# Hop gathers in a graph network: the rows of each group split into two float32r parts for one 256-column product

## What is computed

```python
h = relu(layernorm(x))
msg = where(edge_type == 0, h[src] @ W_data.T + b_data, h[src] @ W_control.T + b_control)
x = x + relu(segment_sum(msg, dst) + h @ W_self.T + b_self)
h = relu(layernorm(x)); out = h
norm = deg_inv_sqrt[src] * deg_inv_sqrt[dst]
for _ in range(2):
    h = segment_sum(h[src] * norm[:, None], dst)
    out = out + h
return x + out / 3
```

## Time and profile before

| | us |
|---|---|
| median of 3 runs (lowest to highest) | 4009.13 (4006.95 to 4013.33) |
| the profiled execution | 4008.96 |
| its span, first to last instruction | 4007.0 |
| TensorE busy (products) | 3415.7 |
| VectorE busy | 2200.8 |
| ScalarE busy | 2418.7 |
| GpSimd busy | 2745.4 |

### The profile page before, as it was taken

One profiled execution on the slowest core, in us unless ns is written; L12 is line 12 of the kernel. 1 busy time (PEld: TensorE's weight loads), 2 busy tenths in 40 slices (PEclk: granted clock), 3 DMA queues, 4 the chain that ended last, 5 costly groups with the idle time before them and its releaser, 6 DMA issues.

```text
span 4007.0 us, 50989 instructions
## 1 busy us (share of the span) xinstructions
PE 3415.7 (85%) x17910; PEld 2466.8 (62%) x17910; DVE 2200.8 (55%) x3265; ACT 2418.7 (60%) x3174; POOL 2745.4 (69%) x2915
## 2 busy tenths in 40 slices
PE   7666777787777778777777899999998899999999
PEld 4344444444444444444444688888887688888887
DVE  7523888888988889898898422222222222122212
ACT  4001444454444445444444688888887788888887
POOL 2677777777777777777777576666664376666664
PEclk9788999899999999999999999999999999999999
DMA  6222443434343444444344566666666666666665
GB/s 194 86 60 61 119 116 110 133 110 125 109 126 109 115 129 117 118 117 117 110 133 109 168 185 190 192 189 191 190 191 182 179 184 182 181 181 182 186 182 145
DMA packets 555542, 581.12 MB, mean 145 GB/s; under 512 B 73206, under 2 KB 408193, under 8 KB 555283
## 3 DMA queue, kind: packets, MB, share of 16 engines
q1 hardware_dynamic: 463315, 390.14, 33.7%
q0 software_dynamic: 91104, 187.29, 17.1%
q10 hardware_dynamic: 864, 0.39, 0.0%
HBM read 428.15 MB, written 149.41 MB: 144 GB/s over the span
## 4 chain that ended last, share of the span: by engine, by line
PE 44%; POOL 38%; issue 12%; DVE 3%; DMA 1%; ACT 1%; DVEq 0%; SPq 0%; POOLq 0%; ACTq 0%
POOL rows L883 37%; PE wide L1184 35%; PE sums_bank L1100 7%; PE wide L1065 1%; DVE stage L1536 1%; ACT strip_ring L1020 1%; DMA stage<-hop_table 1%; POOL stage L923 0%; DVE big L1238 0%; DVE rows L1278 0%; PE wide L1199 0%; PE turned_bank L1135 0%; DMA rows<-typed_table,index 0%; DVE stage L1533 0%; DVE hot L1489 0%
## 5 line engine op out<-in xcount | busy, mean ns | idle before, releaser
L883 POOL DMA_INDIRECT rows<-typed_table,index x1661 | 1590.3, 957 | 506.0 <-issue 505.3
L1020 ACT CAST strip_ring<-stage 128x2048 fp32r<-128x2048 uint8 (+1 forms) x800 | 1438.8, 1869 | 261.0 <-PE wide L1184 250.2
L883 POOL DMA_INDIRECT rows<-hop_table,index x1162 | 1115.5, 960 | 621.6 <-issue 318.7
L1184 PE MATMUL wide<-strip_ring,table_parts 128*128 128x512 f32 x6272 | 1476.9, 394 | 39.6 <-ACT strip_ring L1020 39.6
L1011 ACT CAST stage<-wide 128x392 uint8<-128x392 f32 x2048 | 847.3, 501 | 929.2 <-PE wide L1144 927.2
L1184 PEld LDWEIGHTS wide<-strip_ring,table_parts 128*128 128x128 f32 x6272 | 1177.1, 190 | 283.7 <-issue 21.5
L1135 PE MATMUL turned_bank<-all_twos 128*128 128x512 bf16 x3328 | 1130.8, 393 | 0.0
L1144 PE MATMUL wide<-stage 128*128 128x392 bf16 x2048 | 700.0, 342 | 284.9 <-DVE stage L1536 283.9
L1100 PE MATMUL sums_bank<-rows,hot 128*128 128x129 f32 (+1 forms) x5646 | 743.3, 287 | 218.9 <-DMA rows<-typed_table,index 204.4
L1536 DVE TENSOR_TENSOR stage<-count_up,stage 128x1568 bf16<-128x1568 f32 x512 | 910.4, 1778 | 0.0
L1100 PEld LDWEIGHTS sums_bank<-rows,hot 128*128 128x128 f32 x5646 | 721.8, 202 | 274.6 <-issue 232.4
(11 more groups left out here) (143 smaller groups left out, 706.9 us busy)
## 6 DMA issues: line engine op xcount, KB each, us to landing
stage<-strips SPq DMA_DIRECT2D x768, 256.0 KB, 2.9
strips<-stage SPq DMA_DIRECT2D x64, 1536.0 KB
rows<-typed_table,index POOLq DMA_INDIRECT x1661
rows<-hop_table,index POOLq DMA_INDIRECT x1162
resid<-xin SPq DMA_DIRECT2D x50, 256.0 KB, 3.6
hop_table<-scaled SPq DMA_DIRECT2D x50, 256.0 KB, 4.1
xin<-resid SPq DMA_DIRECT2D x50, 256.0 KB, 3.6
typed_table<-rows SPq DMA_DIRECT2D x49, 256.0 KB, 2.1
```

What stands on the lines that cost most here:

```text
L883: pool.indirect_dma_start(out=rows[:, o % RING, c, 0:P], out_offset=None, in_=tables[k], in_offset=bass.IndirectOffsetOnAxis(ap=index[:, c ...
L1020: act.copy(strip_ring[:, number % STRIP_RING, 0:size], counts_ring[place][:, 0:size]).then_inc(strip_cast, 1)
L1184: last = pe.matmul(in_blocks(wide[:, nth % 2, :]), table_parts[:, b, part, :], moving[:, :, b - blocks[0], :], start=(begins and b == bloc ...
```

## The change

In hops 1 and 2, VectorE no longer leaves the gathered rows as they are. For each group it copies them, rounded to float32r, to a fifth place in the ring (`high`), and then writes the exact difference over the gathered rows (`low`). TensorE then does one float32r product for each chunk instead of a plain float32 one: 256 moving columns, 128 of `high` and 128 of `low`, against the same one-hot matrix, now typed float32r. The two halves land side by side in the PSUM bank, and `add_group` adds both, with four instructions instead of two and a wait between the pairs.

There is one place for `high`, so the split of group o waits until group o-1 is summed, and for the group's rows. It stands at the end of VectorE's iteration for the slot before (the first group's at the end of its own). TensorE's `sum_group` waits for the split. Pass 0 keeps its products.

The fifth place in the ring takes SBUF from the staging area: two of the six buffers for counts move to a part of `index` that is not read any more by then.

```diff
@@ constants
+OLD_PLACES = 2
-STAGE_WORDS = 11264
+STAGE_WORDS = 10240
@@ buffers
-        rows = sbuf("rows", [RING, CHUNKS, TILE])
-        hot = sbuf("hot", [HOT_RING, CHUNKS, P])
+        with nc.sbuf_tensor("rows", [P, RING + 1, CHUNKS, TILE], F32) as rows, nc.sbuf_tensor("hot", [P, HOT_RING, CHUNKS, P], F32) as hot:
+            pass
+        row_parts = sbuf("row_parts", [RING + 1, CHUNKS, TILE], F32R)
+        hot_exact = sbuf("hot_exact", [HOT_RING, CHUNKS, P], F32R)
...
+        old_index = [index[:, n * piece_words // 4:(n + 1) * piece_words // 4].bitcast(U8) for n in range(OLD_PLACES)]
         counts_ring = [region(piece_words // 4, U8, start=table_words + STRIP_RING * piece_words + n * piece_words // 4)
-                       for n in range(COUNT_RING)]
+                       for n in range(COUNT_RING - OLD_PLACES)] + old_index
@@ TensorE
+            def sum_parts(bank, slot, size, hots):
+                both = row_parts[:, slot:RING + 1:RING - slot, :, 0:P]
+                for c in range(size):
+                    last = pe.matmul(sums_bank[:, bank, 0:PARTS * P].rearrange("p (n f) -> p n f", n=PARTS), hots[:, c, :],
+                                     both[:, :, c, :], start=(c == 0), stop=(c == size - 1))
+                return last
...
                     if o >= 2:
                         pe.wait_ge(added, o - 1)
+                    if k:
+                        pe.wait_ge(rows_split, o - groups + 1)
+                        sum_parts(o % 2, slot, size_of(group), hot_exact[:, o % HOT_RING, :, :]).then_inc(summed, 1)
+                        return
                     pe.wait_ge(rows_landed[slot], landed_by[o])
@@ VectorE
+                    into = hot_exact[:, place, :, :] if k else hot[:, place, :, :]
...
+                    for part in range(parts):
+                        if part:
+                            last.then_inc(high_added, 1)
+                            dve.wait_ge(high_added, o - groups + 1)
+                        for n, inside_tile in enumerate((in_upper[:, group:group + 1], in_lower[:, group:group + 1])):
+                            into = flat_sums[:, ds(base - tile_place(first) + n * TILE, columns)]
+                            last = dve.scalar_tensor_tensor(out=into, in0=sums_bank[:, o % 2, part * P:part * P + columns], scalar=inside_tile,
+                                                            in1=into, op0=ALU.mult, op1=ALU.add)
                     last.then_inc(added, 1)
+
+                def split_rows(o):
+                    slot, size = o % RING, size_of(places[o][1])
+                    whole_rows, high, low = rows[:, slot, 0:size, 0:P], row_parts[:, RING, 0:size, 0:P], row_parts[:, slot, 0:size, 0:P]
+                    dve.wait_ge(summed, o)
+                    dve.wait_ge(rows_landed[slot], landed_by[o])
+                    dve.tensor_copy(high, whole_rows).then_inc(rows_high, 1)
+                    dve.wait_ge(rows_high, o - groups + 1)
+                    dve.tensor_tensor(low, whole_rows, high.bitcast(F32), ALU.subtract).then_inc(rows_split, 1)
@@ end of VectorE's iteration i
+                        if k and i == 0:
+                            split_rows(o)
+                        if k and i + 1 < hop_groups:
+                            split_rows(o + 1)
```

More of the change, by code:

```diff
@@ L305, in gnn_kernel @@
         cell_rows = [region(2 * P).rearrange("p (e n) -> p e n", n=2) for _ in range(2)]
+        old_index = [index[:, n * piece_words // 4:(n + 1) * piece_words // 4].bitcast(U8) for n in range(OLD_PLACES)]
+        assert OLD_PLACES * piece_words // 4 <= first_group * CHUNKS
         counts_ring = [region(piece_words // 4, U8, start=table_words + STRIP_RING * piece_words + n * piece_words // 4)
-                       for n in range(COUNT_RING)]
+                       for n in range(COUNT_RING - OLD_PLACES)] + old_index
         reloaded = [region(reload_words) for _ in range(RELOAD_RING)]
@@ L442, in gnn_kernel @@
         sums_copied = semaphore("sums_copied")
+        rows_high = semaphore("rows_high")
+        rows_split = semaphore("rows_split")
+        high_added = semaphore("high_added")
         sums_turned = semaphore("sums_turned")
@@ L1129, in sum_group @@
                         pe.wait_ge(added, o - 1)
+                    if k:
+                        pe.wait_ge(rows_split, o - groups + 1)
+                        sum_parts(o % 2, slot, size_of(group), hot_exact[:, o % HOT_RING, :, :]).then_inc(summed, 1)
+                        return
                     pe.wait_ge(rows_landed[slot], landed_by[o])
-                    sum_rows(o % 2, slot, size_of(group), hot[:, o % HOT_RING, :, :], TILE if k == 0 else P).then_inc(summed, 1)
+                    sum_rows(o % 2, slot, size_of(group), hot[:, o % HOT_RING, :, :], TILE).then_inc(summed, 1)
                 def fill(n):
@@ L1485, in make_hot @@
                 def make_hot(o):
-                    place, group = o % HOT_RING, places[o][1]
+                    place, (k, group) = o % HOT_RING, places[o]
                     if o >= HOT_RING:
                         dve.wait_ge(summed, o - HOT_RING + 1)
-                    dve.tensor_tensor(hot[:, place, :, :], counting(CHUNKS, P),
+                    into = hot_exact[:, place, :, :] if k else hot[:, place, :, :]
+                    dve.tensor_tensor(into, counting(CHUNKS, P),
                                       local[:, group * CHUNKS:(group + 1) * CHUNKS].unsqueeze(2).to_broadcast([P, CHUNKS, P]),
@@ L1507, in add_group @@
                     columns = TILE if k == 0 else P
+                    parts = PARTS if k else 1
                     flat_sums = sums[:, j % 2, :, :].rearrange("p t f -> p (t f)")
[L1509 to L1512, removed]
-                    last.then_inc(added, 1)
+                    for part in range(parts):
[6 more added lines that the diff above has]
+                                                            in1=into, op0=ALU.mult, op1=ALU.add)
+                    last.then_inc(added, 1)
+                def split_rows(o):
[6 more added lines that the diff above has]
+                    dve.tensor_tensor(low, whole_rows, high.bitcast(F32), ALU.subtract).then_inc(rows_split, 1)
                 def cut(j, k, s, o):
```

## The result

The changed kernel takes 3899.35 us (median of 4 runs, 3892.43 to 3900.32) beside 4011.23 us for the kernel before (4006.95 to 4014.53). The ratio is 0.9717, with a 95% interval of 0.9705 to 0.973: 2.8% faster, about 113 us. The forecast was 3910 us, the range 3890 to 3965.

The account below looks back on a forecast made before the run. PE was taken to bound the kernel in both hops. From the profiled 4008.96 us, 102 us came off for the shorter product and 3 us were added at the end: 3910 us, range 3890 to 3965.

Parts of the forecast that it names:

- What bounds: Both hops: PE is busy throughout, so a microsecond of PE is a microsecond of the kernel until another engine is full.
- The product: PE's group sums in the hops: 121 ns a chunk for 212.5, saving 91.5 ns on 1117 chunks, 102 us.
- The 15 ns beyond the columns: Each product on PE: some 15 ns on top of its columns, so 256 columns cost 121.2 ns rather than 106.3.
- The rival in which weight loads set the pace: PE's sums: each product waits for its own 188 ns load, saving only 24 ns a chunk; 3985 us; chance 0.05.
- The split: DVE, each hop group: copy and subtraction take 2.2 us (to 2.6), hidden beside dense steps with 6 us of cover.
- the last six groups: End of hop 1: 45 chunks save nothing, since PE idles after the sum until ACT has made reloaded table parts.
- The end: Last groups of hop 2: the last split and two more pairs of additions are not hidden, +3 us.
- The moved count buffers: Two count buffers at another address: same loads at the same steps, costed at nothing.
- The gathers: POOL's queue in the hops: blocking of 0.8 us a group raises 9.86 us to 10.65, against PE's slot of 10.73.
- Its own rival: POOL's gathers become the bound: gain lost from 0.65 us of blocking a group; 4099 us at 2.0; chances 0.06, 0.03, 0.05.
- A late split in every slot: Hops: PE waits 2.2 us for DVE after each sum, +206 us, 4218 us; chance 0.02.
- No cheaper product: PE's sums: 256 float32r columns cost what 256 plain ones would, 425 ns; +237 us, 4249 us; chance 0.05.

Follow-up runs that it names:

- two pairs: Copy and subtraction done twice for each group, against the changed kernel with one of each: 3971.22 us, ratio 0.99.

## Why the prediction was right

**What bounds.** PE was the bound before and is after; a microsecond taken from it was a microsecond of the kernel. Right, and shown from both sides: the product without the split gives 0.971, the split without the product 1.0001.

**The product.** The new product was put at 121 ns. Eight of them with 284 ns for the last take 1.13 us, so (1.13 - 0.284) / 7 = 121 ns: right. The old one was put at 212.5 ns a chunk, and this term was too small: whole slots show 105 ns saved and not 91.5, so some 226 ns. I had taken the time from the first pass to the start of the next dense product. At the end of that stretch, in the kernel before:

```profile
2416.43 0.27 PE L1100 MATMUL sums_bank<-rows,hot 128*128 128x128 f32 x1
2416.46 0.48 PE L1184 MATMUL wide<-strip_ring,table_parts 128*128 128x512 f32 x1
```

The dense product starts 0.03 us behind the last pass, much closer than passes follow each other, and takes 0.48 us; in the kernel after it starts 0.12 us behind and takes 0.39:

```profile
2400.97 0.39 PE L1203 MATMUL wide<-strip_ring,table_parts 128*128 128x512 f32 x1
```

So 0.09 us of the old sum stood in the row of the dense product, and only the length of whole slots has it. With 105 ns the forecast's own sum is 1117 x 105 = 117, less 3: 3895 us instead of 3910.

The reason given for 121 was half wrong. The 15 ns beyond the columns were to belong to each product; with 128 columns that makes 68 ns, and 113 were measured. 256 columns lie just above a floor that the two smaller products show. That 121 came out right is luck in part: the 106.3 ns for 256 columns were read from plain passes of 128 columns, which cost 113, and no row was given for why a plain pass should cost what 256 float32r columns do. The rival in which weight loads set the pace at 188 ns is out: that is how long a load takes, and the products with their loads came 121 ns apart. Whether loads make the floor of 113 stays open.

**The split.** Hidden in both steady stretches, with the durations forecast: copy 0.71 us (bounds 0.79 and 1.2), subtraction 1.23 (1.21). At the end of hop 1 one split was late, by 5.1 us, where it was to fit or be covered. It cost nothing that shows: from the 67th sum of hop 1 to the first of hop 2 takes 137.8 us, and 137.7 in the run with the product alone, which has no such wait. Before it was 135.6, so the last six groups saved nothing, as costed. The end cost 1.8 us; 3 were forecast. The moved count buffers cost nothing, as said: a cast from them takes 1906 ns, from the others 1905.

**The gathers.** PE was to stay the bound by a hair (10.65 against 10.73): it is 10.51 against 10.62. But this came out by two errors that cancel, and that is luck. The 9.86 us left out the gap of some 0.3 us ahead of the gathers that also waited for a sum. With it, a group took 8 x (0.959 + 0.305) = 10.11 us before. And blocking, put at 0.8 us a group by a random meeting, is 8 x (1.010 - 0.959) = 0.41. With 10.11 and 0.8 the forecast would have had POOL at 10.91 and as the bound. Its own rival says so too, in which gain is lost from 0.65 us on: 140 x (0.8 - 0.65) = 21 us.

POOL's wait went to nothing, as said. The meeting is not random either: how much the copy and the subtraction hold gathers depends on where the gathers stand in time. It was 0.13 and 0.29 us a group in the changed kernel, 0.26 and 0.06 with the split alone, and a second subtraction held one gather in every group. The rival's threshold is borne out: with two pairs the blocking is 8 x (1.112 - 0.959) = 1.22 us, by the rival 140 x (1.22 - 0.65) = 80 us of loss, and 72 were measured.

**The other rivals.** A late split in every slot: PE has no idle time ahead of a sum in either steady stretch. No cheaper product: 121 ns against the 425 it would have needed.

## What to carry to other kernels

Don't price a product by its columns alone: where each product has float32 weights of its own, halving the columns of a plain float32 pass brought nothing here, and merging two passes into one float32r product with twice the columns brought nearly half of the sum's time. Price a stage by the distance between like events a slot apart, not by the start of the next kind of instruction. And before work is put on an idle VectorE beside GpSimd's indirect gathers, work out what is left on GpSimd's queue, with the gap ahead of every gather: it was the nearest bound, though VectorE had 8 us to spare in each slot.

## What the runs showed of the hardware

TensorE products with 128x128 float32 or float32r weights of their own cost no less than 113 ns each, by the length of whole hops: float32r with 128 columns, and plain passes with 128 or with 64 columns. With 256 float32r columns it was 121 ns, with 512 it was 227.6, and plain passes of 384 columns came 325 ns apart. Products of one bf16 column, with weights of their own, came 26 ns apart.

A gather on GpSimd that starts under a two-input VectorE subtraction of 1.22 us takes 1.65 us instead of 0.95, and ends 0.82 us after it; three copies of 0.71 us in a row cost a group's eight gathers 0.15 us more than one. The Trainium skill, SBUF — State Buffer, section "Who interferes with whom", says that a VectorE instruction with two SBUF inputs contends with a GpSimd instruction that reads SBUF. The runs agree with that sentence (1.65 against 0.95 us), if the gather, which takes its row numbers from `index` in SBUF, is such an instruction. The same section reports that `tensor_tensor` did not stall a DMA in a probe; for these gathers the measurement says otherwise. In hop 2 of the changed kernel the subtraction is the dearer of the two: it held gathers for 20.1 us, the copy for 8.8.
